# One core, graph layer and 16-expert layer: the second eight experts' weights are made in blocks 8 to 39 instead of 0 to 31

## What is computed

```python
deg = jnp.maximum((adj != 0).astype(jnp.float32).sum(-1), 1.0)
x = x + gnn(layernorm(x), adj, deg[..., None], W, b)     # relu((a_norm @ h + h) @ W + b)
xf = layernorm(x)                                        # 4096 x 256
probs = softmax(xf @ Wr + br)                            # 4096 x 16
topk_w, topk_idx = top_k(probs, 2)                       # normalised to sum 1
for e in range(16):
    h = gelu(xf @ W1[e] + b1[e], approximate=False)      # 256 -> 512
    o = h @ W2[e] + b2[e]                                # 512 -> 256
    y = y + combine[:, e:e + 1] * o
x = x + xf + y
```

## Times and profile before

| | us |
|---|---|
| median of 3 runs (627.71 to 632.73) | 627.83 |
| the profiled execution | 626.15 |
| its span, first to last instruction | 624.6 |

### The profile page before, as it was taken

One profiled execution on the slowest core, in us unless ns is written; L12 is line 12 of the kernel. 1 busy time (PEld: TensorE's weight loads), 2 busy tenths in 40 slices (PEclk: granted clock), 3 DMA queues, 4 the chain that ended last, 5 costly groups with the idle time before them and its releaser, 6 DMA issues. The chain is left out here.

```text
span 624.6 us, 16840 instructions
## 1 busy us (share of the span) xinstructions
PE 582.1 (93%) x4756; PEld 461.0 (74%) x4756; DVE 461.2 (74%) x1469; ACT 237.1 (38%) x483; POOL 310.0 (50%) x361
## 2 busy tenths in 40 slices
PE   7899999999999999999839998999999999999992
PEld 6687888888888888888715665666677777777772
DVE  5777899999999999999855666666666666566561
ACT  3563443444444334344323444444432333323321
POOL 7333466666666666664342334525334443544343
PEclk9999999999999999999958999999999999999998
DMA  9976999999999999999548435766544543444430
GB/s 223 223 121 154 186 205 213 214 213 203 211 214 210 216 211 207 207 208 243 194 123 306 112 104 99 177 151 140 105 85 74 85 86 65 76 72 83 67 50 1
DMA packets 67605, 95.87 MB, mean 154 GB/s; under 512 B 9312, under 2 KB 42112, under 8 KB 67040
## 3 DMA queue, kind: packets, MB, share of 16 engines
q0 software_dynamic: 33408, 52.42, 48.4%
q1 hardware_dynamic: 32672, 40.88, 22.3%
q10 hardware_dynamic: 1472, 1.88, 0.9%
HBM read 103.71 MB, written 26.94 MB: 209 GB/s over the span
## 5 line engine op out<-in xcount | busy, mean ns | idle before, releaser
L502 PE MATMUL bank<-wall,at_xg 128*128 128x257 f16 x1024 | 238.8, 274 | 4.8 <-DVE at_xg L884 4.4
L504 PE MATMUL bank<-wall,at_xg 128*128 128x256 f16 x1024 | 233.6, 273 | 0.0
L1370 POOL DMA_INDIRECT out_dram<-orows,at_xg x79 | 123.9, 1568 | 161.7 <-DMA out_dram<-orows,at_xg 103.7
L1194 DVE SCALAR_TENSOR_TENSOR hl<-bank,xseT 128x512 f16<-128x512 f32 x79 | 54.6, 691 | 92.1 <-ACT xseT L817 92.1
L811 ACT ACTIVATE hgs<-hgs 128x512 f32<-128x512 f32 x79 | 49.8, 630 | 187.6 <-DVE hgs L1188 187.6
L628 PE MATMUL bank<-wall,feat 128*128 (+1 forms) x474 | 117.4, 385 | 2.1 <-DVE feat L1175 2.1
L502 PEld LDWEIGHTS bank<-wall,at_xg 128*128 128x128 f16 x1024 | 102.8, 100 | 21.6 <-DVE at_xg L884 8.2
L1338 POOL DMA_INDIRECT rows<-feat,posi x64 | 73.4, 1147 | 86.9 <-issue 82.2
L504 PEld LDWEIGHTS bank<-wall,at_xg 128*128 128x128 f16 x1024 | 100.2, 98 | 15.5 <-DVE wall L891 0.3
L654 PE MATMUL bank<-wall,xseT 128*128 (+1 forms) x632 | 108.2, 273 | 0.0
L884 DVE STREAM_TRANSPOSE at_xg<-abuf 128x512 int32<-128x512 int32 x128 | 87.0, 698 | 4.0 <-DVE abuf L876 0.3
(11 more groups left out here) (151 smaller groups left out, 765.0 us busy)
## 6 DMA issues: line engine op xcount, KB each, us to landing
abuf<-in_adj_dram POOLq DMA_DIRECT2D x128, 256.0 KB, 6.4
wst<-in_L_ffn_W_dram SPq DMA_DIRECT2D x32, 512.0 KB, 6.2
at_xg<-rows SPq DMA_DIRECT2D x79, 136.0 KB, 2.4
out_dram<-orows SPq DMA_DIRECT2D x32, 128.0 KB
abuf<-in_L_ffn_b_dram SPq DMA_DIRECT2D x4, 1024.0 KB, 8.2
wall<-in_x_dram SPq DMA_DIRECT2D x10, 256.0 KB, 12.8
rows<-pad POOLq DMA_DIRECT2D x11, 136.0 KB, 6.0
out_dram<-orows,at_xg POOLq DMA_INDIRECT x79
```

The lines of the kernel that those rows point to most:

```text
L502: both = [lambda: pe.matmul(ps_acc[odd][:, 0:D + 1], w, yh[:, j, 0:D + 1], start=j == 0, stop=j == T - 1), lambda: pe.matmul(ps_acc[odd][: ...
L504: lambda: pe.matmul(ps_acc[odd][:, 0:D], w, yl[:, j, :], start=False, stop=False)]
L1194: V.scalar_tensor_tensor(out=hl[:, r % 2, :], in0=q_g[r % 2][:, :], scalar=SH, in1=hh[:, r % 2, :], op0=ALU.mult, op1=ALU.subtract).then_i ...
L1370: L.indirect_dma_start(out, bass.IndirectOffsetOnAxis(ap=info[r][:, 0:1].bitcast(U32), axis=0), orow[r], None, bounds_check=N - 1, oob_is_ ...
```

## The change

`LATE` is 5 instead of 4, so one more round of eight blocks is written out. `late` gives weight (b - 8) // 2 in steps 8 to 39 and nothing in steps 0 to 7. The two first transfers are no longer asked for in the last tile of the graph part but behind blocks 0 to 3 and `b1`.

```diff
-LATE = 4
+LATE = 5
@@
     def late(q, r):
-        return (U * q + r) // 2 if isinstance(q, int) and U * q + r < 4 * (E - EARLY) else None
+        return (U * q + r - U) // 2 if isinstance(q, int) and U <= U * q + r < U + 4 * (E - EARLY) else None
@@ def step(i, k), SyncE
-            if isinstance(t, int) and t == T - 1:
-                load_late(0)
-                load_late(1)
@@ SyncE, after the graph part
         for r in range(AHEAD):
             load_block(0, r)
         load_b1(2)
         load_b1(3)
+        load_late(0)
+        load_late(1)
         over_blocks(sp, bstep)
```

## The result

The changed kernel takes 633.17 us (median of 22 runs, 629.85 to 636.33), the kernel before, run beside it, 629.82 us (median of 22, 626.55 to 632.73). The ratio is 1.0064 (95% interval 1.005 to 1.0078), some 4.0 us slower: less than 1%, but clear. The forecast was 629.7 with a range up to 632.9, made on a median of 627.83 from three runs. Of the 3.5 us by which the time misses it, 2.0 are that median, which was low; the rest is that the change costs more than the forecast 1.9 (3.4 by the two medians, 4.0 by the ratio).

A forecast was written before the change was run, and what follows sets the result against it. TensorE bounds the free stretch, a ScalarE-VectorE ring the late-work steps, serial adds the blocks up to 17. +3.6 us (steps 32 to 39) and -1.7 (block 17) give +1.9: 629.7 us on the 627.83 median, range 626.5 to 632.9.

The forecast's parts named there:

- The start, steps 0 to 4: Start of the expert part: add 0 starts 0.9 us earlier; block 4 lands at 341.4, TensorE waits 2.5 us.
- lower bound of 1.0 us: SyncE's queue ahead of block 4: at least the issue time of two weight transfers, 1.0 us, is lost.
- The clock: TensorE after the block 4 wait: waits of 1.56 and 1.27 us left full speed, so 2.5 us may too.
- rival C: The block 4 wait lowers TensorE's clock for some 6 us: 3.0 us of work lost, time 632.7; chance 0.12.
- The chain of adds: Serial adds of blocks 0 to 9: add 1 starts 0.2 us later, adds gain 2.0, block 17 at 389.3.
- The relief: Adds 1 to 5 lose three late-weight transfers beside them: up to 3.1 us or next to nothing, taken as 2.0.
- -1.7: Net shift at block 17: the later of 389.3 by the adds and 389.4 by TensorE, against 391.07 before.
- The waits at blocks 16 and 17: TensorE waits 1.56 and 1.27 us for tokens in the kernel before, 2.83 us together, where computing catches up with the adds.
- the ring: ScalarE and VectorE wait for each other in turn: about 3.79 us a turn with a late half weight, 3.19 without.
- Steps 32 to 39: Eight blocks get late work at 0.45 us each: +3.6 us, bounds 3.3 and 4.8.
- A: The chain of adds is not relieved: block 17 0.2 us later, plus 3.6, time 631.6; chance 0.20.
- nothing moves by more than 1%: Whole kernel: no change beyond about 1% (6.3 us), chance 0.92; slower by that 0.06, faster 0.02.

The follow-up runs named there:

- transfers behind the blocks: Changed kernel with its first two weight transfers asked for behind the loads of blocks 4 to 7, not ahead of them; ratio 1.0057 to the kernel before.
- eighteen matmuls: Changed kernel with eighteen unused 512-column matmuls on TensorE ahead of the transposes of block 4; ratio 1.005 to the kernel before.
- kernel before with five rounds: Kernel before with LATE = 5 and nothing else, late work still in blocks 0 to 31; ratio 0.9986 to the kernel before.
- old place: Changed kernel with its first two weight transfers back in the last tile of the graph part; ratio 1.0035 to the kernel before.
- run without early adds: Late work in 8 to 39, first transfers in the graph part's last tile, results of blocks 0 to 7 written aside, not added; ratio 0.9985 to kernel before.
- ten matmuls: Changed kernel with ten unused 512-column matmuls on TensorE ahead of the transposes of block 4; ratio 1.0071 to the kernel before.
- 16 to 47: Late work in blocks 16 to 47, six rounds written out, first transfers behind the loads of blocks 4 to 7; ratio 1.0057 to the kernel before.
- 0 to 31, half in the gap: Kernel before with VectorE's half weight moved one step later, between bias1 and cut_low, five rounds written out; ratio 0.9953 to the kernel before.
- 16 to 47, half in the gap: Late work in 16 to 47, VectorE's half between bias1 and cut_low, seven rounds, transfers behind blocks 4 to 7; ratio 0.9914 to kernel before.

## Why the prediction was wrong

**The start, steps 0 to 4: right in kind, 0.5 us off.** Add 0 starts 0.8 earlier (forecast 0.9). TensorE has the tokens of block 4 at 345.32 - 328.90 = 16.4 from T0, forecast 341.4 - 325.5 = 15.9; it waited 2.83 us, forecast 2.5. The rule on ring order (the Trainium skill, "DMA: Bandwidth & Descriptors", "Queues, rings and completion order") says that on each DMA engine descriptors are consumed in ring order. These runs agree: with the same transfers behind the blocks there is no wait. Two small slips stand in the forecast's sum here: by a whole megabyte (3.9 us) block 4 lands at 342.5, so that the sum would be 1.1 us higher and not 0.9, and at the lower bound of 1.0 us TensorE would come to it 0.45 us later than before and not 0.7. Neither changes what follows.

**The clock: judged wrong, but it did not decide.** The forecast took it that the clock would outlast the wait, since 1.56 and 1.27 us had left it alone, and gave rival C 0.12. It fell, and cost 1.7 us at block 4 (the rival had 3.0). The Trainium skill, "TensorE: Matmul & The Clock Gate", "HAM oscillation — how this bites in real kernels", says that an idle stretch in a wait for a transfer sends the clock back to half; the 2.83 us agree, a wait of 2.95 us in another kernel here does not. So which way the clock went at this wait was in part luck. And little of the 1.7 us arrives: against the run with eighteen matmuls 0.6 us are left at block 17. There TensorE waits another 1.47 us for tokens, which it would not do if its own work set the pace.

**The chain of adds: the step that failed.** The forecast had "block 17 by the chain: 391.07 + 0.2 - 2.0 = 389.3", which is 63.8 from T0. TensorE has these tokens at 394.79 - 328.90 = 65.9, 2.1 us later, and after a wait, so it is the chain that sets them. The 2.1 us have three parts:

- Add 1 starts at 21.4 from T0 and not at 20.6: 0.8. Block 4 came 0.5 later than forecast, and the step behind it ran in part at the low clock.
- The relief, "I take 2.0", is 1.5: from add 1 to add 9 it takes 387.08 - 350.33 = 36.75 us against 38.26 before. The forecast counted three transfers of weights as a burden on adds 1 to 5. Only the one beside add 4 shows (6.37 us to the next add with it, 5.42 in the kernel before with five rounds, 4.67 to 4.81 in the seven kernels without it); beside add 2 a transfer changes nothing in these two kernels (4.84 and 4.65 with it, 4.64 to 4.81 without). From add 1 to add 5 the kernel with five rounds takes 18.2 us with all its transfers, the one at the old place 18.9 without them.
- From add 9 to the tokens of block 17 it takes 394.79 - 387.08 = 7.7 us, before 391.07 - 384.20 = 6.9: 0.8. The forecast took this as unchanged, without a reason. Why it is longer is open.

So add 9 is 0.5 us earlier than before where the sum wanted 1.8, block 17 comes 0.3 later where the sum wanted -1.7, and the clock is not what took it: where it did not fall at block 4 (transfers at the old place, or behind, or eighteen matmuls), the gelu of block 17 comes at +0.4, +0.4 and -0.3. (In the first two it fell later, after a wait for tokens that an add held up.) Nor does an early add 1 help: it starts anywhere from 19.1 to 22.0 us after T0 in the five kernels with late work in 8 to 39 and adds, and add 9 from 57.9 to 58.8. The mechanism, that what is saved before block 17 is lost in the waits for the adds, was stated in the forecast and was right, and the run without early adds shows it: 5.2 us. The forecast had the chain as one of two limits that meet at block 17 (389.3 and 389.4). In every kernel here that has the adds and comes to block 8 early, TensorE waits for tokens at block 16 or 17, so there the chain is the later one.

**The waits at blocks 16 and 17** are 2.83 us of idle TensorE, but only some 1.1 us of the end, since TensorE idles there part of the time anyway while the ring is slower. It did not change the sum, but it made the possible gain look larger.

**Steps 32 to 39: right, 3.6 forecast, 4.0 measured.** The pace of 3.83 came from twelve steps; over steps 17 to 31 it is 3.86, one of them 4.28, and the first free steps behind a late stretch run at 3.33 and not at 3.38, as VectorE catches up. That is 0.5 us for each block and not 0.45.

**The sum.** -1.7 became +0.3, and 3.6 became 4.1: +4.4 in the profile, 4.0 by the ratio. Rivals A (+3.8) and C (+4.9) lie on both sides of it. A's outcome is nearest, block 17 0.2 us late and 3.6 more behind it, but not A's sign: it wanted over 4 us of waiting at blocks 16 and 17, and 1.47 were there. Of C there is the fall of the clock. That nothing moves by more than 1% was right.

## What to carry to other kernels

A stretch in which a slower chain (here the adds) runs beside the computing gives little back for work that is taken out of it (here nothing for eight blocks, 1.9 of some 7 us for sixteen), while the place to which the work goes pays in full: look first for the stretch that has another bound, and put the work there. In a ring of two engines an instruction costs its time at one place of the queue and nothing at another: 32 halves moved into the wait of VectorE for ScalarE, behind the chain of adds, made the kernel 0.9% faster, where moving them by eight blocks made it 0.6% slower. And a transfer that is asked for early stands ahead of the one that is needed early.

## What the hardware showed that was not expected

The clock fell in the middle of dense work after waits of TensorE for tokens of 2.83 us (changed kernel), 2.25 (ten matmuls), 2.50 (old place), 2.08 (transfers behind the blocks), 2.67 (16 to 47), and 2.89 and 2.35 (0 to 31, half in the gap). It held after every wait for tokens up to 1.56 us. But it also held after one of 2.44 us (transfers behind the blocks, 11 us after the one of 2.08 that lowered it), and after the longest of all, 2.95 us (16 to 47, half in the gap, block 16, with the stages around and behind it):

```profile
387.90 0.40 PE L602 MATMUL bank<-id,at_xg 128*128 128x128 f16 x4 [2.95 <-DMA at_xg<-rows]
...
384.00:388.00 4.00, 1.05 (x7) 0.32 (x6) 1.08 (x2) 0.00 (x1) 3.03 (x2) 1.00 0.50 75
388.00:392.00 4.00, 4.00 (x35) 2.92 (x35) 2.35 (x5) 1.11 (x2) 1.82 (x2) 1.00 0.47 90
```

So between 2.08 and 2.95 us the length of the wait alone does not decide; what else does is not shown.

Block 4's load was asked for 0.6 us after T0 in the kernel before (326.07) and landed 13.1 us after T0. In the changed kernel SyncE's issues are (L385 the two weights, L424 the blocks behind them)

```profile
329.51 1.93 SPq L385 DMA_DIRECT2D wst<-in_L_ffn_W_dram  x2
331.48 2.61 SPq L424 DMA_DIRECT2D at_xg<-rows  x2
```

so block 4 is asked for 2.6 us after T0 and lands 13.1 us later, 15.7 after T0. Of the 2.6 us by which it is late, 2.0 had passed before it was asked for: the two issues of weights took 1.93 us in a busy queue, where the forecast gave them 1.0. So the megabyte cost most of its time before the load it delays was even in the queue.

An add of 128 rows of 1 KB that waits for the one before takes on average 4.8 us from start to start in the kernel before, and 4.5 in adds 1 to 9 with no transfer of weights beside them ((54.9 - 19.1) / 8, late work in 16 to 47). It takes 5.2 where the halves stand in the gap in blocks 0 to 31 ((61.5 - 14.4) / 9). These are paces of the chain: some of the adds start when VectorE's `weigh` is done and not when the add before has landed.
